# The end of the first attention: conditioning through folded weights, sums in a bank of their own, VectorE taking one eviction and one rounding

## The reference

```python
def _L0_attn_ref(x, Wq, Wk, Wv, Wo, quantum_phase, quantum_amplitude):
    ...                                       # 16 heads of 8 features
    w = jax.nn.softmax(scores * cos_mat, axis=-1)
    w = (w + jnp.roll(w, 1, axis=-1)) / math.sqrt(2.0)
    out = jnp.einsum('bhij,bhjd->bhid', w, v)
    return out.transpose(0, 2, 1, 3).reshape(B, S, d) @ Wo

def _L0_cond2_ref(x, y, weight, mask, bias):
    w_bot = jnp.einsum('bg,got->bot', y, weight * mask[None, :, :])
    return jnp.einsum('bnt,bot->bno', x, w_bot) + bias

def _L0_ffn_ref(x, w_gate, w_up, w_down):
    def act_qdq(x):                           # one scale for the whole tensor
        scale = jnp.maximum(jnp.max(jnp.abs(x)) / 32767, 1e-12)
        return jnp.clip(jnp.round(x / scale), -32768, 32767) * scale
    x = act_qdq(x)
    up = act_qdq(x @ lpbq_dequant(w_up).T)
    gate = act_qdq(x @ lpbq_dequant(w_gate).T)
    ...

x = x + _L0_attn_ref(_L0_cond_ref(x, ...), ...)
x = x + _L0_ffn_ref(_L0_cond2_ref(x, cond_8, ...), ...)
```

## Time and profile before

| what | us |
|---|---|
| median of 3 runs | 1321.96 (1321.25 to 1324.37) |
| the profiled execution | 1317.24 |
| its span | 1315.4 |
| `norm` of the last sequence ends | 148.19 |
| first gate product starts | 155.57 |

### The profile page before, as it was taken

How to read it: one execution, slowest core, us unless ns; L and a number is a source line. 1 busy time by engine, 2 the same in 40 slices (tenths; PEclk the granted TensorE clock), 3 DMA queues, 4 the chain that set the end, 5 groups by cost and what they waited for, 6 DMA issues and landing times.

```text
span 1315.4 us, 28323 instructions
## 1 busy us (share of the span) xinstructions
PE 1208.6 (92%) x10403; PEld 968.8 (74%) x10403; DVE 825.7 (63%) x1741; ACT 648.0 (49%) x1326; POOL 273.7 (21%) x355
## 2 busy tenths in 40 slices
PE   5999876889999899999999999899999999988999
PEld 2767522558888799887888888499889876656777
DVE  6878698555565667567776565566564577754342
ACT  2778675354443334443444444234434367656553
POOL 5667200200014134220000023144230022100000
PEclk9999997999999999999999999999999999999999
DMA  9000200510502232105025001032111000000000
GB/s 333 4 2 2 81 1 8 208 65 1 216 5 91 61 108 68 33 19 217 1 91 235 1 11 47 27 115 71 35 38 65 1 3 3 3 2 0 1 16 16
DMA packets 42900, 75.85 MB, mean 58 GB/s; under 512 B 3849, under 2 KB 33809, under 8 KB 41873
## 3 DMA queue, kind: packets, MB, share of 16 engines
q1 hardware_dynamic: 38672, 65.66, 13.8%
q0 software_dynamic: 4096, 8.40, 2.2%
HBM read 59.75 MB, written 14.29 MB: 56 GB/s over the span
## 4 chain that ended last, share of the span: by engine, by line
PE 72%; DVE 16%; ACT 6%; issue 3%; DVEq 1%; DMA 1%; POOL 0%; ACTq 0%; SPq 0%; POOLq 0%
PE banks L1967 8%; PE banks L1978 7%; PE banks L1963 7%; PE banks L2022 5%; PE banks L1954 4%; PE banks L2032 3%; PE banks L1700 3%; PE banks L1705 3%; PE banks L1707 3%; PE banks L1706 3%; PE banks L1947 2%; PE banks L1949 2%; PE banks L1948 2%; PE banks L1831 2%; PE banks L1790 1%
## 5 line engine op out<-in xcount | busy, mean ns | idle before, releaser
L2226 ACT ACTIVATE SC<-banks 128x512 f32<-128x512 f32 x192 | 114.4, 596 | 225.6 <-PE banks L1963 127.9
L2313 DVE SCALAR_TENSOR_TENSOR SC<-banks,SM,SC 128x512 f32<-128x512 f32 x128 | 95.8, 748 | 122.1 <-PE banks L1967 102.2
L1978 PE MATMUL banks<-A,SC 128*128 x1024 | 137.0, 277 | 7.8 <-DVE SC L2313 7.1
L1967 PE MATMUL banks<-X,SC 128*128 128x128 f32 x1024 | 137.6, 278 | 3.7 <-DVE SC L2588 3.2
L1963 PEld LDWEIGHTS banks<-X,SC 128*128 128x128 f32 x1024 | 126.5, 192 | 19.6 <-issue 12.3
L1963 PE MATMUL banks<-X,SC 128*128 128x128 f32 x1024 | 136.7, 277 | 4.4 <-ACT SC L2210 3.2
L1978 PEld LDWEIGHTS banks<-A,SC 128*128 128x128 f32 x1024 | 125.4, 192 | 17.3 <-issue 16.4
L1967 PEld LDWEIGHTS banks<-X,SC 128*128 128x128 f32 x1024 | 125.4, 193 | 6.1 <-DVE SC L2588 5.8
L2022 PE MATMUL banks<-A 128*128 128x128 f32 x736 | 99.5, 278 | 11.2 <-DVE A L2738 5.9
L2022 PEld LDWEIGHTS banks<-A 128*128 128x128 f32 x736 | 89.3, 191 | 15.6 <-ACT A L2251 9.0
L2210 ACT ACTIVATE SC<-A 128x512 f32 x128 | 80.6, 630 | 28.2 <-PE banks L1967 22.6
(11 more groups left out here) (345 smaller groups left out, 2523.7 us busy)
## 6 DMA issues: line engine op xcount, KB each, us to landing
A<-in_moe SPq DMA_DIRECT2D x36, 768.0 KB, 10.0
A<-xs SPq DMA_DIRECT2D x20, 256.0 KB, 3.5
ys<-A SPq DMA_DIRECT2D x20, 256.0 KB, 2.3
BW<-in_l1f SPq DMA_DIRECT2D x2, 2048.0 KB, 7.9
BW<-in_l2f SPq DMA_DIRECT2D x1, 3456.0 KB, 12.1
BW<-in_l1c SPq DMA_DIRECT2D x1, 3072.0 KB, 17.4
BW<-in_l3f SPq DMA_DIRECT2D x1, 2816.0 KB, 9.6
A<-in_l1c SPq DMA_DIRECT2D x1, 2560.0 KB, 8.6
```

The source lines that it names most:

```text
L1967: m = e.matmul(at["pu"].ap[:, cut(q)], wx[:, cut(4 + q)], x, start=True, stop=True)
L1978: m = e.matmul(o, at["h"].ap[:, cut(q)], W[:, bass.ds(r + (1024 + 128 * q), 128)], start=k == 0 and q == 0, stop=k == 1 and q == 3)
L2226: e.activation(at["h"].ap, at["pg"].ap, ACT.Gelu_apprx_tanh).then_inc(at["gelu"][0], 1)
L2313: return e.scalar_tensor_tensor(out=o, in0=a, scalar=s, in1=b, op0=o1, op1=o2)
```

## The change

The last chunk's conditioning is written as WBOT (X + o0 o) = WBOT X + (WBOT o0) o. Two products are issued ahead of the transposes of (15, 1): `wfold`, which multiplies the four conditioning matrices of chunk 3 by the transposed output weights `o0T` (a new constant of 128 columns), and `cond2_x`, which multiplies the old `X` of chunk 3 by `WBOT`. ScalarE evicts both behind the last `turn` (`fold_out`), the second with the bias into `Y`. After the last `norm`, `cond2_o` multiplies `o` by the folded weights, and VectorE adds this to `Y`. `att_out` comes behind it, and its addition to `X` is done between the reduction on VectorE and the use of GpSimd's result (`x0_later`).

For the last sequence the sums go to a bank of ring `RA`, and those of the first half are issued in the first `pv` step. VectorE evicts the first four transposes of (15, 1), ScalarE the second four. `y_max(2)` is moved from ahead of the last `norm` to behind `cond2_o`'s addition. `keep_on(4)` becomes `keep_on(6)`. Chunk 0 is rounded in both operations by VectorE.

```diff
-         ("q0a", 128), ("k0a", 128), ("v0", 128), ("trig", 128), ("maskT", 128), ("o0", 128),
+         ("q0a", 128), ("k0a", 128), ("v0", 128), ("trig", 128), ("maskT", 128), ("o0", 128), ("o0T", 128),
...
+                                st["ps", j] = RA.take() if (n, j) == (3, 3) else None
...
+                                if at["later"]:
+                                    sig["x0_later"] = later
+                                else:
+                                    add()
...
             def first_half(p):
-                if p:
+                if p == 16:
+                    fold_begin()
+                    parts[15, 1][1](by=("vec", "act"))
+                    fold_end()
+                elif p:
                     parts[p - 1, 1][1]()
...
                 if p == 16:
-                    for n in range(3):
-                        y_max(n)
+                    y_max(0)
+                    y_max(1)
...
                 if p == 16:
+                    cond2_o(chunk[3]["o"], chunk[3]["to"])
                     parts["out", 3]()
+                    y_max(2)
...
+        def fold_begin():
+            at = step("wfold", wbot=sig["wb", 12], pa=RA.take())
+            at["mm"] = tick("c2_mm")
+            bt = step("cond2_x", pa=RA.take())
+            bt["mm"] = tick("c2_mm")
+            fold.update(w=at, x=bt)
...
+        def cond2_o(o, to):
+            at = step("cond2_o", w=fold["to"], ready=fold["w"]["t"], yx=fold["x"]["t"], o=o, to=to, pa=RA.take())
+            at["mm"] = sig["wbot_over"] = tick("c2_mm")
+            at["y"] = sig["y0b", 3] = tick("c2_add")
+            RA.give(at["pa"], at["y"])
...
-        items.append(([("x0", 3)], [lambda: cond2(3, RA)], ("y0b", 3)))
...
-        keep_on(4)
+        keep_on(6)
         at = step("f0_magic")
         t_mag = tick("f0_vec")
         y_max(3)
-        scl, inv, t = scale_of(mx, 4, sig["ymax"])
+        scl, inv, t = scale_of(mx, 4, sig["ymax"], (), sig["x0_later"])
...
+                    own = at["ps"] is not None
+                    sums = at["ps"].ap[:, 0:128] if own else pc[:, 128:256]
+                    if own:
+                        over(at["ps"])
+                    for g in range(2 * at["half"], 2 * at["half"] + 2) if own else range(4 if at["half"] else 0):
...
                 elif kind == "f0_yq":
-                    w.wait_ge(*at["act"])
                     w.wait_ge(*at["ready"])
+                    if at["n"] == 0:
+                        ts(ch(Y, 0), ch(Y, 0), at["inv"], MAGIC, ALU.mult, ALU.add).then_inc(at["q"][0], 1)
+                    w.wait_ge(*at["q"])
                     ts(ch(Y, at["n"]), ch(Y, at["n"]), MAGIC, at["scl"], ALU.subtract, ALU.mult).then_inc(at["t"][0], 1)
```

More of the change, by code:

```diff
@@ L548, in s_norm @@
                             (RC if i else RC0).give(st["pc", j], at["t"])
+                            if at["ps"] is not None:
+                                RA.give(at["ps"], at["rcp"])
                         def s_soft(s_max=s_max, s_exp=s_exp):
@@ L731, in cond2, with fold_end @@
             ring.give(at["pa"], at["y"])
+        fold = {}
+        def fold_begin():
[4 more added lines that the diff above has]
+            fold.update(w=at, x=bt)
+        def fold_end():
+            at, bt = fold["w"], fold["x"]
+            ct = step("fold_out", w=at, x=bt, to=RWB.take(), yfree=sig["Yfree", 3])
+            at["t"], bt["t"] = tick("c2_fold"), tick("c2_y")
+            RA.give(at["pa"], at["t"])
+            RA.give(bt["pa"], bt["t"])
+            fold["to"] = ct["to"]
+        def cond2_o(o, to):
[3 more added lines that the diff above has]
+            RA.give(at["pa"], at["y"])
         def y_max(n):
@@ L791, in build @@
             at = step("f0_yq", n=n, scl=scl, inv=inv, ready=t)
[L792 removed]
+            at["q"], at["t"] = tick("f0_act" if n else "f0_vec"), tick("f0_vec")
             tq.append(at["t"])
@@ L1851, in _ @@
                         m = e.matmul(at["pa"].ap[:, cut(j)], WBOT[:, b, :], X[:, b, :], start=True, stop=True)
+                    m.then_inc(at["mm"][0], 1)
+                elif kind == "wfold":
+                    over(at["pa"])
+                    w.wait_ge(*loaded["cst2"])
+                    w.wait_ge(*at["wbot"])
+                    e.matmul(v4(at["pa"].ap), c("o0T"), WBOT[:, 12:16, :], start=True, stop=True).then_inc(at["mm"][0], 1)
+                elif kind == "cond2_x":
+                    over(at["pa"])
+                    for j in range(4):
+                        m = e.matmul(at["pa"].ap[:, cut(j)], WBOT[:, 12 + j, :], X[:, 12 + j, :], start=True, stop=True)
+                    m.then_inc(at["mm"][0], 1)
+                elif kind == "cond2_o":
+                    over(at["pa"])
+                    w.wait_ge(*at["ready"])
+                    w.wait_ge(*at["to"])
+                    for j in range(4):
+                        m = e.matmul(at["pa"].ap[:, cut(j)], at["w"].ap[:, cut(j)], at["o"].ap[:, cut(j)], start=True, stop=True)
                     m.then_inc(at["mm"][0], 1)
@@ L2147, in _ @@
                     e.activation(ch(Y, at["n"]), v4(at["pa"].ap), ACT.Identity, bias=c("c2b")).then_inc(at["y"][0], 1)
+                elif kind == "fold_out":
+                    over(at["to"])
+                    w.wait_ge(*at["w"]["mm"])
+                    e.activation(at["to"].ap, at["w"]["pa"].ap, ACT.Identity).then_inc(at["w"]["t"][0], 1)
+                    w.wait_ge(*at["x"]["mm"])
+                    w.wait_ge(*loaded["cst2"])
+                    w.wait_ge(*at["yfree"])
+                    e.activation(ch(Y, 3), v4(at["x"]["pa"].ap), ACT.Identity, bias=c("c2b")).then_inc(at["x"]["t"][0], 1)
                 elif kind == "f0_magic":
@@ L2423, in _ @@
                     e.tensor_tensor(v4(at["s"].ap[:, 0:4 * k]), pa[0], bc_last(m[:, 0:4], k), ALU.add).then_inc(at["sub"][0], 1)
+                elif kind == "turn" and "vec" in at["by"]:
+                    over(at["p"])
+                    for x, pb in enumerate(at["pb"]):
+                        if at["by"][x] == "vec":
+                            w.wait_ge(*at["tr"][x])
+                            e.tensor_copy(at["p"].ap[:, 512 * x:512 * x + 512], pb.ap).then_inc(at["t"][x][0], 1)
                 elif kind == "norm":
@@ L2428, in _ @@
                     w.wait_ge(*at["pv"])
-                    e.reciprocal(at["rr"].ap, pc[:, 128:256]).then_inc(at["rcp"][0], 1)
+                    sums = pc[:, 128:256] if at["ps"] is None else at["ps"].ap[:, 0:128]
+                    e.reciprocal(at["rr"].ap, sums).then_inc(at["rcp"][0], 1)
                     w.wait_ge(*at["rcp"])
                     e.tensor_tensor(at["o"].ap[:, cut(j)], pc[:, 0:128], at["rr"].ap, ALU.mult).then_inc(at["t"][0], 1)
-                elif kind == "att_out":
+                elif kind == "att_out" and not at["later"] or kind == "att_add":
+                    at = at.get("of", at)
                     w.wait_ge(*at["mm"])
                     e.tensor_tensor(ch(X, at["n"]), v4(at["pa"].ap), ch(X, at["n"]), ALU.add).then_inc(at["x"][0], 1)
+                elif kind == "cond2_o":
+                    w.wait_ge(*at["mm"])
+                    w.wait_ge(*at["yx"])
+                    e.tensor_tensor(ch(Y, 3), v4(at["pa"].ap), ch(Y, 3), ALU.add).then_inc(at["y"][0], 1)
                 elif kind == "wmask":
@@ L2993 @@
         "q0a": I["L0_attn_Wq"][:, twice], "k0a": I["L0_attn_Wk"][:, twice], "v0": I["L0_attn_Wv"],
-        "o0": I["L0_attn_Wo"][spread],
+        "o0": I["L0_attn_Wo"][spread], "o0T": I["L0_attn_Wo"][spread].T,
         "maskT": I["L0_cond2_mask"].T, "c2b": col(I["L0_cond2_bias"]),
```

34 lines of the change are left out of this document (19 added, 15 removed).

## The result

The changed kernel takes 1323.59 us (median of 22 runs, 1319.57 to 1326.95) where the kernel before takes 1319.90 (22 runs, 1316.03 to 1324.37). The ratio is 1.0031 with a 95% interval of 1.0022 to 1.0040: 4.1 us slower, 2.9 to 5.3 (the medians differ by 3.7). That is on the edge of the 0.3% that the prediction set as its bound, and larger than the 0.6 us of its sum. The change was therefore measurably slower, on the side that the sum gave and by several times its size, while the time itself lay within the range.

The account below looks back on a forecast made before the run. It took a chain of waits from norm to the first up product, with TensorE's queue deciding after the change, as the bound; +0.44 there and +0.18 at the start, about +0.6 on 1321.96, gave 1322.6 us, range 1318.5 to 1326.5.

Parts of the forecast that it names:

- the 0.6 us of its sum: Whole kernel: +0.44 us at the first up product plus +0.18 at the start, +0.62, said as +0.6.
- TensorE's queue decides after `norm`: From norm's end to the first up product: conditioning, att_out and twelve identity records take 7.02 us, outlasting the data.
- data path: From norm's end through conditioning, addition, maxima, reduction and roundings to the first up product: 5.8 us, against 7.38 before.
- the rounding on VectorE and the addition in the pause: Between norm and the first up product: both worth nothing, ending 1.2 us before anyone wants them.
- Rival 1: After norm: the six identity products do not bind and the data path does, -0.6 us, 1321.4; chance 0.08.
- The fold delays the last transposes: Ahead of the (15, 1) transposes: wfold and cond2_x make them start at 144.70, not 143.58, 1.12 us late.
- from 142.76 + 0.11 the two end at 144.70: TensorE's queue: wfold (0.86 us) and cond2_x (0.97) start one transpose's place after the last transpose's start at 142.76.
- rival 2: Ahead of the last transposes: the fold is hidden in TensorE's gaps, giving 1321.5 us; chance 0.10.
- 65.5 KB at 373 GB/s: At the start: o0T lengthens the constants' transfer ahead of the one the angles wait for, adding 0.18 us.
- I carry it to the end of the kernel: After the first up product: a late TensorE start at 155.57 is late one for one through to the end.
- Rival 3: In the gap 147.65 to 149.02: TensorE's clock falls, keep_on takes 10.3 us, not 5.2, giving 1327.8; chance 0.05.
- Rival 4: At 185 to 215 us: a low-clock stretch moves or shortens, making the kernel over 0.3% (4 us) faster; chance 0.07.

Follow-up runs that it names:

- e1_keep4: The changed kernel with four products of the identity instead of six; ratio to the kernel before 0.9992 (0.9980 to 1.0005).
- e7_fold_behind: The changed kernel with wfold, cond2_x and their evictions moved behind TensorE's last products; ratio to the kernel before 1.0002 (0.9990 to 1.0014).
- e9_three_more: The kernel before with three more VectorE instructions writing constants nobody reads; ratio to the kernel before 1.0013 (1.0000 to 1.0026).
- e3_load_only: The kernel before with the 128 columns of o0T, unread, added to its second load; ratio to the kernel before 0.9994 (0.9985 to 1.0003).
- e8_keep1: The changed kernel with one product of the identity instead of six; ratio to the kernel before 1.0020 (1.0006 to 1.0034).

## Why the prediction was right, and where its sum was short

**TensorE's queue decides after `norm`.** Right, and shown by three runs: six products on the old order (+0.71), four on the new (-1.45), three with the rest put right. The prediction had 7.02 us from `norm`'s end to the first up product, the profile 7.12. Its data path, 5.8, was 5.60 in e1_keep4. So the rounding on VectorE and the addition in the pause were worth nothing in the changed kernel, as forecast. Rival 1 is refuted.

**The fold delays the last transposes.** Right; the size was 1.39 and not 1.12, or 1.34 against the exponentials, which ended 0.05 later. The step that was off is "from 142.76 + 0.11 the two end at 144.70". `wfold` began at 143.12, 0.25 later than that step had it, these 0.05 included. `norm` ended 1.01 later against the exponentials and not 0.80. e7_fold_behind takes that away in full (-1.23), so rival 2, a fold hidden in gaps, is refuted.

**The end of the attention in sum.** +0.66 us by the last gate eviction, +0.44 in the forecast.

**The start.** "65.5 KB at 373 GB/s", 0.18 us, was too little: 0.75 in the profiled pair, 0.5 over twelve profiles. The spread between kernels with the same loads is 0.6, which one profile can't tell. The clock then blurs it: in the changed kernel's profile the shift was +0.74 at 12 us and +0.05 at 60, since it spent less of the time near 31 us at the low level: the granted clock from 26 to 42 was 0.89, where the kernel before had 0.79.

**The step that failed: "I carry it to the end of the kernel".** The forecast held that what is late at 166 is late by the same amount at the end, and nothing else moves. From the same instruction in both profiles, the shift is:

```
at (us, kernel before)   12     60    170   240   290   350   430   500   820   862   910   end
changed less before    +0.74  +0.05 +0.72 +0.70 +0.99 +0.97 +1.32 +1.71 +1.68 +2.81 +3.51 +3.30
```

Flat for hundreds of microseconds, with steps. The step between 350 and 430 is VectorE's pause at 388, and about 0.4 of the step from 820 to 862 is the other. The rest of that step goes with one more stretch at the low clock: the granted clock from 850 to 862 was 0.86 in the changed profile and 1.00 in the one before. The steps from 430 to 500 and from 862 to 910 were not traced to a cause. The prediction priced what three more VectorE instructions cost where they stand, and not that they renumber some 2900 behind them. That is the missing term: 0.8 us by the two pauses on the chain, 1.7 (0 to 3.4) by e9_three_more's time, 1.5 at equal clock. With 0.66 for the attention's end and 0.5 for the start, the sum is 2.0 to 2.9 us, against 4.1 (2.9 to 5.3) and 2.9 (0.7 to 5.0), or 2.3 ± 0.9 at equal clock, which it meets. Of this, the 0.5 is read from the profiles only; e3_load_only's time does not show it.

**Where luck came in.** The forecast was 1322.6 and the median 1323.6, but this nearness is owed to two errors that offset each other. The sum was added to the median of three runs, 1321.96, where 22 runs gave 1319.90, so the base was 2.1 too high while the effect was 3.1 to 3.5 too small. And the range was 8 us wide for the spread of executions, not for missing terms.

**What stays open.** 1 to 2 us of the 4.1, and how much belongs to the clock. Later falls of the clock come and go with the moment (near 448, 598, 834, 855 and 1185 us, in some profiles and not in others). The mean granted clock over the runs was 0.9845 for the changed kernel, and 0.986 to 0.987 for the kernel before in the experiments' runs; at 0.7 us for each 0.001 that would be an estimated 1.1 to 1.4 us, most of what is open. Whether the change brings more such stretches or met them by chance is not settled: all eight experiments with three more VectorE instructions had a lower mean clock than the kernel before beside them, by 0.0001 to 0.0027, but e3_load_only without them did too, by 0.0001, and the larger differences are few. Rival 3 did not occur in the changed kernel's gap in any of its profiles: the granted clock from 140 to 170 was 1.00. Rival 4 did not occur either: from 185 to 217 it was 0.63 in the changed profile and 0.68 in the one before, so the low stretch had not shrunk. Nor do the parts add up exactly in the variants. For e1_keep4 they give -0.79 + 0.5 for the load + 0.8 to 1.7 for the pauses, +0.5 to +1.4 us, where -1.1 was measured (-2.6 to +0.7); for e7_fold_behind +1.1 to +2.0 where +0.3 was measured (-1.3 to +1.8). Both favour the lower price of the pauses, and so do their estimates at equal clock, 0.7 for e7_fold_behind and -1.6 for e1_keep4; the latter stays unexplained by any price.

**The chances.** 0.88 for no change and 0.07 for slower were too sure. 0.3% was taken for what a measurement tells from no change; 22 runs of each told it to 0.09%. A sum of 0.6 left over 3 us of room to the bound, but that room was judged by the terms in the sum, while 1150 us of kernel stood behind the change without any term at all.

## What to carry to other kernels

Work put into a gap of a queue in order has to be compared with the gap: here 1.83 us of products went into 0.55 and delayed everything behind, while a gap of 1.3 us under the reciprocal, a few instructions later, was free. The same goes for filler that keeps the clock up: too much of it becomes the bound the moment that the data path gets shorter, too little may let the clock fall (e8_keep1, one profile), so size it again with each change of the path. And when a small local change is timed, repeat the kernel before with as many idle instructions added to the same queue; what that costs is not the merit or fault of the idea.

## What the runs showed of the hardware that was not expected

VectorE's queue can pause for 0.40 to 0.43 us before every 128th of its records, numbers 63, 191, 319 and so on. Seven of the 24 places show it in each of the twelve profiles: the same seven in the nine kernels with three more instructions, and one other set of seven in the three without. In four profiles where they were looked at, the other engines' queues show no such period. Many of the other places lie where the queue waits for a semaphore or runs ahead of a long operation. Of those that show it, some lie on the chain of waits. Three more instructions early on move four of the seven. The Trainium skill ("Runtime: NRT & Kernel Launch", "Instruction fetch mechanics") has instructions fetched in blocks of 256 and the fetch hidden behind issue; these rows show a period of 128 records and a pause that is not hidden. The page of the changed kernel has the transfers of instructions:

```profile
q8 instruction: 89, 1.46, 0.5%
q14 instruction: 43, 0.35, 0.1%
```

Those of q14 are of 8192 bytes, which is 64 for each of 128 records, and lie 30 us apart on average. By the packets of the traces, one of them starts behind each of the 84 pauses in the twelve profiles, 0.67 to 1.6 us after its end (three times 2.2 to 2.5). So the pause stands where one block of 128 ends, and the transfer follows it. Since it starts only after the pause, the pause is not the wait for that transfer; what the queue does in it was not shown by any run.

TensorE's clock fell once in a gap that, in two other profiles of the same order, it lived through at 1.00: e3_load_only from 150.6 us on, against the kernel before and e9_three_more. In all three TensorE had been idle for about 1.4 and 0.9 us just ahead.
